# One wait per piece of 56 writes, in place of four element writes under way at most

## What is computed

```python
edge_index = jnp.stack([src, dst])
x = _layernorm(x + _L0_gnn_ref(x, edge_index, ...))               # GCN, three steps
x = _layernorm(x + _L1_gnn_ref(x, edge_index, edge_weight, ...))  # attention, four heads
x = _layernorm(x + _L2_gnn_ref(x, edge_index, ...))               # SAGE, two steps
x = _layernorm(x + _L3_gnn_ref(x, edge_index, ...))               # mean over the source's edges, two steps

# a step of the first kind
h = x @ W
msg = h[src] * norm[:, None]
out = jax.ops.segment_sum(msg, dst, num_segments=num_nodes)
```

## Time and profile before

| | before |
|---|---|
| three timed runs, median (lowest to highest) | 5740.17 us (5734.01 to 5756.72) |
| profiled execution | 5702.34 us |
| its span, first to last instruction | 5700.5 us |
| TensorE's granted clock, mean | 0.865 of full speed |
| busy, share of the span | PE 58%, PEld 54%, DVE 49%, POOL 36%, ACT 29% |
| clearing the matrix, last DMA issued | 283 us |
| element writes | 109 to 1238 us |
| pass 0 | from 1274 us |

### The profile page before, as it was taken

The page is one execution under the profiler, slowest core; times in us unless marked ns, Lnnn a source line. Parts: engine busy times, 40 slices in busy tenths (PEclk is TensorE's granted clock), DMA queues, the critical chain, the costliest instruction groups (busy, mean ns, idle before and its releaser), DMA issues.

```text
span 5700.5 us, 61044 instructions
## 1 busy us (share of the span) xinstructions
PE 3324.1 (58%) x19159; PEld 3100.7 (54%) x19160; DVE 2808.7 (49%) x3801; ACT 1675.3 (29%) x2774; POOL 2048.7 (36%) x1982
## 2 busy tenths in 40 slices
PE   1300000019999999544444444357479999689697
PEld 0300000019999999544333343246379789589597
DVE  8300000024454544677666677788954344544345
ACT  0000000005645455200000000023266356456265
POOL 2777666750000000377677777346300000200300
PEclk9999999999999999755555555579789999799798
DMA  9700000008858587499899899247368268478585
GB/s 356 275 1 16 1 1 1 1 12 278 257 183 276 175 275 227 126 228 220 215 216 214 215 221 222 62 122 214 92 205 277 84 208 277 151 244 285 180 283 183
DMA packets 887483, 1008.44 MB, mean 177 GB/s; under 512 B 391651, under 2 KB 651705, under 8 KB 887270
## 3 DMA queue, kind: packets, MB, share of 16 engines
q1 hardware_dynamic: 795778, 861.50, 51.6%
q0 software_dynamic: 56208, 63.97, 4.8%
q10 hardware_dynamic: 35284, 80.30, 3.6%
HBM read 692.09 MB, written 233.14 MB: 162 GB/s over the span
## 4 chain that ended last, share of the span: by engine, by line
PE 44%; another core or an unknown queue 23%; DVE 14%; issue 11%; POOL 3%; ACT 2%; DMA 2%; DVEq 1%; SPq 0%; ACTq 0%; POOLq 0%
PE banks L918 35%; PE banks L841 4%; POOL work L624 2%; PE banks L1000 2%; DVE Z L1397 1%; DVE big L1519 1%; DVE Z L1402 1%; PE banks L863 1%; ACT banks L779 1%; DVE big L1406 1%; DMA work<-tab,stage 1%; DVE Z L1404 1%; ACT X L668 1%; PE banks L966 1%
## 5 line engine op out<-in xcount | busy, mean ns | idle before, releaser
L918 PE MATMUL banks<-wides,rows 128*128 128x384 f32 (+2 forms) x11040 | 2028.5, 344 | 155.8 <-issue 88.6
L918 PEld LDWEIGHTS banks<-wides,rows 128*128 128x128 f32 x11040 | 1949.4, 189 | 229.1 <-issue 94.3
L624 POOL DMA_INDIRECT work<-tab,stage x832 | 902.8, 1085 | 1483.0 <-ACT stage L771 1232.2
L1265 DVE CAST wides<-big 128x768 fp32r<-128x768 f16 (+3 forms) x1429 | 811.1, 569 | 1176.7 <-PE banks L918 1072.3
L698 ACT CAST wides<-big 128x768 fp32r<-128x768 f16 (+2 forms) x1037 | 832.2, 804 | 677.9 <-PE banks L918 554.3
L598 POOL DMA_INDIRECT cells<-queue_i x784 | 787.0, 1004 | 311.9 <-issue 298.6
L972 PE MATMUL banks<-V,work 128*128 x1664 | 372.5, 414 | 378.6 <-ACT work L773 312.1
L972 PEld LDWEIGHTS banks<-V,work 128*128 128x128 f32 x1664 | 345.1, 316 | 415.9 <-issue 415.9
L650 POOL DMA_INDIRECT V<-tab,nodei x100 | 96.2, 962 | 1201.9 <-DMA tab<-X 879.8
L863 PE MATMUL banks<-work 128*128 128x50 f16 x784 | 92.1, 278 | 670.6 <-issue 600.5
L863 PEld LDWEIGHTS banks<-work 128*128 128x128 f16 x784 | 73.1, 149 | 689.5 <-issue 612.6
(11 more groups left out here) (300 smaller groups left out, 3229.1 us busy)
## 6 DMA issues: line engine op xcount, KB each, us to landing
big<-cells SPq DMA_DIRECT2D x490, 416.0 KB
big<-cells SPq DMA_DIRECT2D x441, 384.0 KB
big<-turned SPq DMA_DIRECT2D x300, 384.0 KB
gathered<-work SPq DMA_DIRECT2D x104, 512.0 KB
work<-gathered SPq DMA_DIRECT2D x104, 512.0 KB, 4.2
big<-turned SPq DMA_DIRECT2D x100, 416.0 KB
cells<-work ACTq DMA_DIRECT2D x98, 416.0 KB, 14.6
turned<-big SPq DMA_DIRECT2D x50, 800.0 KB
```

Source lines behind the costliest of these rows:

```text
L624: pool.indirect_dma_start(msg[:, j, u, :], None, tab[0][:, :], bass.IndirectOffsetOnAxis(ap=stage[:, j * U + u:j * U + u + 1].bitcast(U32) ...
L918: last = pe.matmul(banks[:, 4 * (w % 2) + j, 0:(z - a) * P], rows2[:, s, part * D:(part + 1) * D], wides[:, q % QUEUE, (a - start) * P:(z ...
L1265: dve.tensor_copy(wides[:, (2 * m + 1) % QUEUE, 0:(z - a) * P], halves[:, m % HALVES, a * P:z * P]).then_inc(s_wided, 1)
```

## The change

`AHEAD` becomes 8 and gets another meaning. The wait before each write is gone. All 56 writes of a piece add to one semaphore, `s_scat[b % 2]`, by the parity of the piece. At the ninth write of piece b, GpSimd waits once, until all writes of piece b - 1 have landed (16 x 56 for each piece of that parity so far); then it counts `s_written` and starts the next fetch, both of which stood at the fifth write. SyncE and the end of the scatter wait for two semaphores instead of four, each with half of all increments.

```diff
-AHEAD = 4
+AHEAD = 8
...
-        s_scat = [sem(f"s_scat{j}") for j in range(AHEAD)]
+        s_scat = [sem(f"s_scat{j}") for j in range(2)]
...
-        SETTLED = 16 * COLS // AHEAD
+        SETTLED = 16 * COLS // 2
...
-                            for j in range(AHEAD):
+                            for j in range(2):
                                 sp.wait_ge(s_scat[j], SETTLED)
...
                     for u in range(PIECE):
-                        n = b * PIECE + u
-                        if n >= AHEAD:
-                            pool.wait_ge(s_scat[n % AHEAD], 16 * (n // AHEAD))
                         if u == AHEAD:
                             if b:
+                                pool.wait_ge(s_scat[(b - 1) % 2], 16 * PIECE * ((b - 1) // 2 + 1))
                                 pool.sem_inc(s_written, 1)
                             if b + 1 < PIECES:
                                 fetch(b + 1)
                         pool.indirect_dma_start(cells[:, :], bass.IndirectOffsetOnAxis(ap=queue_i[:, b % 2, u:u + 1].bitcast(U32), axis=0),
-                                                queue_i[:, b % 2, PIECE:RECORD].bitcast(H16)[:, u:u + 1], None).then_inc(s_scat[n % AHEAD], 16)
+                                                queue_i[:, b % 2, PIECE:RECORD].bitcast(H16)[:, u:u + 1], None).then_inc(s_scat[b % 2], 16)
...
             scatter(1, PIECES)
-            for j in range(AHEAD):
+            for j in range(2):
                 pool.wait_ge(s_scat[j], SETTLED)
```

More of the change, by code:

```diff
@@ L64, in build @@
     assert ROWQ * 256 == NC and DUMP % 256 == 0 and NPAD < 8191 and NC <= 8192 and COLS <= 2048
-    assert sum(FIRST) == CT and sum(SWEEPS) == CT and sum(BACKS) == TILES and COLS % PIECE == 0 and PIECE % AHEAD == 0
+    assert sum(FIRST) == CT and sum(SWEEPS) == CT and sum(BACKS) == TILES and COLS % PIECE == 0 and PIECES % 2 == 0
     ctx = ExitStack()
```

## The result

On the chip on which the kernel before was timed, the kernel after takes 5796.47 us in the median of five executions (5786.50 to 5798.31, and one execution of 8219.38 us in a slow state, which is left out of this range and of the ratio). The kernel before takes 5740.17 there, also in five (5734.01 to 5756.72). The medians are 56 us apart. The ratio is 1.0088, with a 95% interval of 1.0066 to 1.011: slower by 0.9%. The profiled execution took 5786.5 us with a span of 5784.7, against 5702.34 and 5700.5.

What follows compares the result with a forecast made beforehand. Bound: PE retires one instruction per 1.40 us during POOL's unpaused stream, delaying VectorE's chain. POOL's end 1227, plus 15, 53 and 37 us, gives 1332 instead of 1248.99: +83 us, 5740 to 5823; forecast 5790 to 5845, range 5705 to 5850.

Steps and rivals of the forecast that it cites:

- (4): Counting loop beside the first piece: without POOL's pauses, PE's slow stretch begins before the loop, 22.4 us per half; +83 us.
- POOL's pace: Whole scatter: 206 operations at 1.27 us until 370 us, then 612 at 1.40 us, ending at 1227 us.
- B: Rival, counting loop: slow stretch begins only with the gathers, at 182 us; +13 us, 5753; 0.28 together with C.
- C: Rival, scatter: early onset, but POOL not slowed to 1.40 us, ending at 1148; +7 us, 5747; 0.28 together with B.
- D: Rival, scatter: onset as in B and POOL at 1.27 us throughout; -47 us, 5693; 0.15 with its like.
- The pause behind POOL's end: After the scatter's last write: 11 to 27 us until PE is free, taken as 15, so 1242 us.
- The halves left: Counting loop at 1242 us: 52 of 98 halves done, 46 left at 1.15 us, 53 us, to 1295.
- The tail: Between the counting loop and line 1230: copies, transposes and matmuls take 37 us without lags, reaching it at 1332 us.
- (1): POOL's scatter: removing 780 waits; those met at once cost nothing, at most 22 us over 728 writes.
- (2): First piece of 56 writes: at 1.27 us each it takes 71 us instead of 90, gathers start 18 us earlier.
- (3): Ninth write of each piece: the one wait for the previous piece's landing costs nothing.
- The reading of the 298.6 us: POOL's idle time named "issue" before the scatter writes: a small gap of 0.30 us, present even without waits.

Runs made afterwards that it cites:

- i1: The kernel before, unchanged, profiled on a fifth chip, where the counting loop is not slowed: 5163.52 us, ratio 0.9991.
- g1: The kernel before with AHEAD 8 in place of 4, still one wait ahead of each write: 5161.77 us, ratio 0.9998.
- e1: The kernel before with its cap of four kept only for the first piece and the first four writes of each later piece: 5159.46 us, ratio 0.9995.
- e2: The kernel after, with POOL waiting at every fourth write until all writes of the piece have landed: 5458.60 us, ratio 1.0572 to the kernel before.
- h1: The kernel after with landing waits at every fourth write in the first two pieces and between gather groups: 5222.84 us, ratio 1.0116 to the kernel before.
- f1: The kernel after, word for word, timed again on a second chip: 5152.27 us, ratio 0.9976 to the kernel before.

## Why the prediction was right

It was right for the chip on which it was asked, and in these steps:

- *The onset (4).* The forecast put it at the start of the loop, 125 us, with four halves until 162. The trace has three halves at the free pace and the fourth at 142.13 us, then one per 22.4 us. My "some 5 halves" up to 199 us are six (the three, and 142.13, 164.08 and 186.51).
- *POOL's pace.* The sum had 206 operations up to 370 us and then 1.40 us each. Up to 370 us the trace has 206, and 162 in the 224 us behind it (1.38). The last write was forecast at 1227 us and comes at 1225.15. The slowing that it put at 370 us shows between 370 and 398, and in the kernel before between 454 and 482: its time goes with the start of the unpaused stream (109 and 197 us), as the sum had it. Two rivals fall with this: B, whose onset waits for the gathers, and C, which has POOL end at 1148. D falls with them.
- *The pause behind POOL's end.* I took 15 us until PE is free and it is 11 (1236.5 instead of 1242).
- *The halves left.* Forecast 46 at 1.15 us, 53 us. They are 45 at 1.07 us: 1236.5 to 1285.2, 48.7 us. The 1.15 came from the window of the earlier trace rows with 65 halves; i1 has 70 in the same 74.50 us. In the kernel before DVE was already held up in it by PE, for 1.29 us at 132.61 and 1.25 us at 141.06, so that window held some of the lag, pauses or not.
- *The tail.* Forecast 37 us, and it is 34.8 (1285.17 to 1319.96).

Together these are 12 us, the difference between the forecast 1332 for line 1228 and its 1319.96. The first sweep was forecast at 1357 and stands at 1345.15, 71 us behind the kernel before.

One thing was right by luck, and one was wrong. The luck is the profiled span: it grew by 84 us and I had forecast 83, but only 71 of them come from the scatter. The other 13 arise in and behind the gather phase of lines 624 and 622: its first gather is 70 us later than before (2420.3 against 2350.4), its last 75 (3698.2 against 3622.7), and the first sweep behind it 83 (4260.53 against 4177.35). There too POOL streams in bursts and PE answers late, and the phase takes 1272 us on the first chip and 1140 in i1, so I take the 13 us for variation of the same lag between executions. That was not tested. The sum had taken everything behind the scatter as unchanged. What was wrong is the offset of 38 us between the profiled run and the median, which I carried over. In the kernel after it is 10 us (5786.5 against 5796.47). That is why the median came out at 5796 and not at 5823, by far the largest miss of the forecast: the 12 us of the terms above are made up for by the 13, and the 27 us are this offset. The profiled execution of the kernel before was 32 us faster than the fastest of its five timed ones, so the 84 us between the profiles overstate the 56 between the medians.

Minor points: (1), the removed waits, at nothing, holds within 3.4 us (g1). (2), the shorter first piece, was 72 us where the sum had 71. (3), the new wait, at nothing, holds: no wait of the trace stands at a ninth write. The reading of the 298.6 us as a gap of 0.30 us was too simple: 768 of those would be 230 us, and i1, where POOL doesn't slow down, has 232.9 us in 743. The rest belongs to the slowed stretch.

The rule about 2 us of fixed cost from the Trainium skill's page "DMA: Bandwidth & Descriptors", section "Anatomy of one DMA", fits the landing of the last write (2.16 us in e1) and fails in the clearing. There the cap of four still bound, 13.3 us in 16 waits and 20.5 us in 32 in i1, and a wait of the drains lasted up to 5.7 us (e2).

**What is shown and what isn't.** The two traces from the first chip show that the slow stretch begins behind the start of POOL's first run without pauses, wherever the code puts that (197 us before, 109 us after; the loop starts at 125), and that it ends 11 us behind its last write in both. That the amount lost is the number of halves left at POOL's end, with the tail behind them, follows from the same traces. The experiments show that the stream alone doesn't make PE lag: the same instructions beside the same writes leave the loop at 1.07 us a half and dense matmuls at their pace. Something in the first chip, or in how it was set up, has to come with it. Which of the two isn't known: the record numbers the five chips and not the first, and none of the experiments ran there. My reason, the missing pauses, was not put to the test by an experiment, since no run met the lag; the expectations for such a chip stand above for whoever meets one. A rival that the two traces don't part from it is the stream's pace, 1.27 us an operation without the pauses and 1.58 with them. The pace of an instruction per 1.40 us with PE busy for 4% of the time would fit a shared path by which the engines report what they have finished, and which POOL's stream fills; this is a guess. The Trainium skill's page "NOTIFIC — the notification-queue block", section "7.1 Overflow: three behaviours, one of which stalls the engine", describes one path of that kind, the one that carries notification records, and says of its stall counter that "a nonzero value would mean the notification path had throttled an engine". No run here shows that it is this one. The cause stays open at this point.

**Which version is best.** Without the lag it is the kernel after, by the one chip on which it was timed (5152.27 us, 0.9976 of before), on the first chip the kernel before. No run made one that beats both on both. The kernels with pauses that might stop the lag cost 71 (h1) to 306 us (e2) over the kernel after where there is none.

## What to carry to other kernels

When a chain on other engines runs beside a stream of indirect transfers from GpSimd, look at which of the two ends last, and whether the other engines' instructions keep the duration that they have without the stream. If they don't, what is left to do when the stream ends decides the time, and a cap on the stream that seems to cost 13 us may be what lets a loop run ahead of it. A time from one chip can have the wrong sign for the others: time a small change on more than one before it is kept or dropped, and compare whole executions, since 71 us in one stage of two profiles can be 56 in the medians.

## What the runs showed of the hardware

- The same program takes 5740 us on one chip and 5161 to 5167 us on five others. By the profiles, 314 us of that lie before line 841's first x378, 132 in the gather phase and 94 from the first gather of the last layer on: the three stages in which GpSimd issues indirect transfers.
- Where the lag holds, dense matmuls have it too: 52 in 60 us beside 50 gathers, against 309 in i1.
- The granted clock doesn't explain the loop's lag. In the windows from 566.9 to 790.9 us it is 1.00 on the first chip, with PE lagging, and 0.52 in i1, the lower of TensorE's two levels, where PE waits for the pieces. The slower clock is on the faster chip.
- A landing takes 2.1 us in quiet stretches (median of i1). During the clearing, 29 writes of e1 that waited for the fourth write before them started 6.0 to 7.5 us behind its start. A drain of all writes costs 1.7 to 1.9 us on average, not the 1.0 that the quiet landing suggests.
- An indirect write of 64 indices takes 0.89 us, one of 128 takes 0.97. The price is the instruction's, hardly the elements'.
- Beside a busy DVE about every third of POOL's writes is 0.48 us longer (1.45 instead of 0.97; 14 of 45 in f1).
